# Four graph attention layers on one core: both masks from a transposed adjacency that the host lays beside the first

## What is computed

```python
# layer 0: attention with one head, mask as it is
e = leaky_relu(h @ W.T @ a1 + (h @ W.T @ a2).T); x += elu(softmax(where(adj == 0, -1e9, e)) @ h)
# layer 1: two GAT layers (L1a: 4 heads of 256, elu behind it; L1b: 1 head of 512), softmax over the source
e = leaky_relu(asrc[:, :, None] + adst[:, None, :]); attn = softmax(where(mask, e, -1e9), axis=1)
# layer 2: one head, mask as it is; layer 3: 8 heads of 64 on x @ W_proj, relu behind it
```

## Time and profile before

| | us |
|---|---|
| median of 3 runs (3081.10 to 3087.44) | 3084.61 |
| the profiled execution | 3083.84 |
| its span, first to last instruction | 3082.1 |
| PE busy | 2976.9 (97%) |
| DVE, ACT, POOL busy | 2480.0, 2319.9, 2263.2 |

### The profile page before, as it was taken

One profiled execution on the slowest core, in us unless ns is written; L12 is line 12 of the kernel. 1 busy time (PEld: TensorE's weight loads), 2 busy tenths in 40 slices (PEclk: granted clock), 3 DMA queues, 4 the chain that ended last, 5 costly groups with the idle time before them and its releaser, 6 DMA issues. The chain is left out here.

```text
span 3082.1 us, 79166 instructions
## 1 busy us (share of the span) xinstructions
PE 2976.9 (97%) x21040; PEld 2746.1 (89%) x21040; DVE 2480.0 (80%) x8101; ACT 2319.9 (75%) x6433; POOL 2263.2 (73%) x3214
## 2 busy tenths in 40 slices
PE   7899999999999999999999999999999999999974
PEld 5789999999999999999999999999999999999964
DVE  3578888888888888888888888888888888888852
ACT  2567787778877788777787778877788777787752
POOL 3467777777777777777777777777777777777753
PEclk6999999999999999999999999999999999999985
DMA  5123333333333333333333333333333333333332
GB/s 195 34 69 123 117 119 122 108 124 118 119 123 106 125 117 119 122 109 122 118 119 121 108 122 120 120 118 112 121 120 119 118 110 122 120 120 119 96 107 93
DMA packets 205558, 355.71 MB, mean 115 GB/s; under 512 B 51904, under 2 KB 117568, under 8 KB 188736
## 3 DMA queue, kind: packets, MB, share of 16 engines
q1 hardware_dynamic: 205120, 350.66, 34.8%
HBM read 314.93 MB, written 35.59 MB: 114 GB/s over the span
## 5 line engine op out<-in xcount | busy, mean ns | idle before, releaser
L1454 POOL TENSOR_SCALAR rs<-mv,rs 128x1 f32<-128x1 f32 x512 | 357.6, 698 | 109.2 <-POOL rs L1451 108.8
L997 ACT ACTIVATE eT<-eT,tc 128x128 f32<-128x128 f32 x1024 | 314.1, 389 | 161.3 <-POOL eT L1534 161.3
L432 PE MATMUL bank_b<-w_hi,hT_hi 128*128 128x344 f32 x1536 | 419.8, 328 | 5.6 <-DVE g L1277 3.8
L432 PE MATMUL bank_c<-w_hi,g_hi 128*128 128x258 f32 x2048 | 414.1, 283 | 4.7 <-DVE x L1204 4.7
L432 PE MATMUL bank_c<-w_lo,g_hi 128*128 128x258 f32 x2048 | 414.5, 284 | 0.0
L432 PE MATMUL bank_b<-w_lo,hT_hi 128*128 128x344 f32 x1536 | 408.2, 320 | 0.0
L1329 DVE CUSTOM_DVE_ANT_0 t_all_L<-t_all_L,mask 128x128 f32<-128x128 f32 x1024 | 368.6, 413 | 27.0 <-DMA t_all_L<-t_dram_L 26.5
L432 PE MATMUL bank_b<-w_hi,hT_lo 128*128 128x344 f32 x1536 | 357.0, 327 | 0.0
L432 PE MATMUL bank_c<-w_hi,g_lo 128*128 128x258 f32 x2048 | 351.8, 284 | 0.0
L432 PE MATMUL bank_e<-w_hi,hT_hi 128*128 128x264 f32 x1024 | 341.1, 347 | 5.5 <-DVE out_sb L1372 5.4
L1540 POOL TENSOR_TENSOR eT<-eT,shift_all 128x512 f32<-128x512 f32 x256 | 331.1, 1294 | 4.6 <-ACT eT L997 4.4
(11 more groups left out here) (158 smaller groups left out, 8577.5 us busy)
## 6 DMA issues: line engine op xcount, KB each, us to landing
shift_all<-shift_dram SPq DMA_DIRECT2D x128, 1024.0 KB, 5.3
t_all_L<-t_dram_L SPq DMA_DIRECT2D x128, 512.0 KB, 3.7
x_in<-in_x SPq DMA_DIRECT2D x128, 256.0 KB, 2.6
t_all_L1a<-t_dram_L1a SPq DMA_DIRECT2D x128, 256.0 KB, 3.2
out<-out_sb SPq DMA_DIRECT2D x128, 256.0 KB, 3.1
t_all_L<-t_dram_L SPq DMA_DIRECT2D x256, 64.0 KB, 3.1
adj_in<-in_adj SPq DMA_DIRECT2D x128, 64.0 KB, 3.0
t_dram_L1a<-t_rows_L1a SPq DMA_DIRECT2D x512, 0.5 KB
```

Of the source, the lines that this page charges most:

```text
L432: last = mm(bank[:, 0:width], a[:, c * P:(c + 1) * P], w[:, c, b * width:(b + 1) * width], start=(first and c == chunks[0] and n == 0), st ...
L997: last = activation(eT[:, k, :], eT[:, k, :], ACT.Prelu, bias=tc3[:, k:k + 1], alpha=SLOPE)
L1454: ts(b, mv[layer][:, 0:1], r, -1.0, ALU.mult, ALU.mult).then_inc(sem(f"rs_made{layer}"), 1)
```

## The change

The host stacks the adjacency and its transpose into one array, so that a row of the DMA holds both. `adj_in` and `mask` have two halves, which one `make_mask` fills: half 0 is the mask, half 1 its transpose. A new `turn_mask` on POOL takes the diagonal out of half 1 and writes `mask_turned`; `masked_L3` reads half 1 itself. The two transposes on PE, the two copies on ACT, `identb` and their semaphores are gone. `SKEW` is 11, and the lists of all five engines are put in another order; where a call moves over the end of a step, its graph number changes by one with it (`residual_L0(3)` at the start of a step and `residual_L0(2)` at the end of the one before are the same).

```diff
-SKEW = 12
+SKEW = 11
...
-        identb = sb("identb", [P, P], BF16)
...
-        adj_in = sb("adj_in", [P, XR, P], I32)
-        mask = sb("mask", [P, MR, P], BF16)
+        adj_in = sb("adj_in", [P, XR, 2, P], I32)
+        mask = sb("mask", [P, MR, 2, P], BF16)
         mask_loop = sb("mask_loop", [P, LR, P], BF16)
         mask_turned = sb("mask_turned", [P, TR, P], BF16)
-        mask_flat_turned = sb("mask_flat_turned", [P, PR, P], BF16)
...
                 load(t.graph(0))
-                store(t.graph(12))
                 spread_L2(t.graph(7))
+                send_shift_L3(t.graph(10))
+                send_L1b(t.graph(5))
                 send_L0(t.later_graph(2))
+                spread_shift_L3(t.graph(10))
+                spread_L1b(t.graph(5))
                 spread_L0(t.later_graph(2))
-                send_L1b(t.graph(5))
-                send_shift_L3(t.graph(10))
-                spread_L1b(t.graph(5))
-                spread_shift_L3(t.graph(10))
                 send_L1a(t.graph(3))
+                send_L3(t.graph(9))
                 spread_L1a(t.graph(3))
-                send_L3(t.graph(9))
+                spread_L3(t.graph(9))
+                store(t.graph(11))
                 send_L2(t.graph(6))
-                spread_L3(t.graph(9))
...
-            def turn_mask(t, g):
-                if g.live:
-                    pe.wait_ge(sem("masks_made"), g.made())
-                    if t.full:
-                        pe.wait_ge(sem("x1_made"), g.made())
...
-                    mm(bank_a[:, 0:P], mask_loop[:, g.slot(LR), :], identb[:], start=True, stop=True)\
-                        .then_inc(sem("mask_turned"), 1)
...
-            def turn_mask_L3(t, g):
-                if g.live:
-                    pe.wait_ge(sem("mask_made"), g.made())
-                    if t.full:
-                        pe.wait_ge(sem("mask_copied"), g.made(-7))
...
-                    mm(bank_a[:, 0:P], mask[:, g.slot(MR), :], identb[:], start=True, stop=True)\
-                        .then_inc(sem("flat_turned"), 1)
...
-                project_L1b_first_high(t, t.graph(5))
                 project_L1b_first_low(t, t.graph(5))
+                turn_h3(t, t.graph(9))
                 project_L1b_last(t, t.graph(5))
-                turn_mask(t, t.graph(3))
-                turn_h3(t, t.graph(9))
+                product_L3_last(t, t.graph(11))
                 turn_prob_L1a(t, t.graph(4))
-                product_L3_last(t, t.graph(11))
+                product_L3_first(t, t.graph(11))
                 turn_h1(t, t.graph(3))
-                turn_mask_L3(t, t.graph(10))
                 product_L1a_last(t, t.graph(4))
                 product_L1a_first(t, t.graph(4))
-                product_L3_first(t, t.graph(11))
                 project_L1a_last(t, t.graph(3))
                 turn_exp_L2(t, t.graph(7))
                 project_L3_last_high(t, t.graph(9))
+                project_L3_last_low(t, t.graph(9))
                 product_L2(t, t.graph(7))
-                project_L3_last_low(t, t.graph(9))
                 project_L1a_high(t, t.graph(3))
                 turn_exp_L1b(t, t.graph(5))
+                project_L1a_low(t, t.graph(3))
                 turn_exp_L0(t, t.later_graph(2))
-                project_L1a_low(t, t.graph(3))
                 product_L1b(t, t.graph(5))
+                project_L3_first(t, t.graph(9))
                 product_L0(t, t.later_graph(2))
-                project_L3_first(t, t.graph(9))
+                project_L1b_first_high(t, t.graph(4))
...
-            def copy_mask(g):
-                if g.live:
-                    act.wait_ge(sem("mask_turned"), g.made())
-                    act.wait_ge(sem("L1b_masked"), g.made(TR))
-                    activation(mask_turned[:, g.slot(TR), :], bank_a[:, 0:P], ACT.Copy).then_inc(sem("mask_copied"), 1)
...
-            def copy_mask_L3(g):
-                if g.live:
-                    act.wait_ge(sem("flat_turned"), g.made())
-                    act.wait_ge(sem("L3_masked0"), g.made(PR))
-                    act.wait_ge(sem("L3_masked1"), g.made(PR))
-                    activation(mask_flat_turned[:, g.slot(PR), :], bank_a[:, 0:P], ACT.Copy).then_inc(sem("flat_copied"), 1)
...
-                leaky_L3_first(t.graph(11))
                 leaky_L1a(t.graph(4))
-                norm_0(t.later_graph(2))
-                exp_L1a(t.graph(4))
                 values_L3(t.graph(10))
                 exp_L3_last(t.graph(11))
+                exp_L1a(t.graph(4))
+                hT_hi_L3(t.graph(9))
+                norm_0(t.later_graph(2))
+                exp_L3_first(t.graph(11))
                 norm_1(t.graph(3))
                 pT_L1a(t.graph(4))
-                copy_mask(t.graph(3))
-                hT_hi_L3(t.graph(9))
+                hT_hi_L1a(t.graph(3))
                 leaky_L2(t.graph(7))
-                hT_hi_L1a(t.graph(3))
-                exp_L3_first(t.graph(11))
+                elu_last(t.graph(4))
+                exp_L2(t.graph(7))
                 elu_first(t.graph(4))
-                exp_L2(t.graph(7))
-                copy_mask_L3(t.graph(10))
-                elu_last(t.graph(4))
                 pT_L2(t.graph(7))
-                leaky_L0(t.later_graph(2))
                 g_hi_first(t.graph(4))
-                g_hi_last(t.graph(4))
-                exp_L0(t.later_graph(2))
                 leaky_L1b(t.graph(5))
                 norm_2(t.graph(6))
                 exp_L1b(t.graph(5))
+                g_hi_last(t.graph(4))
+                leaky_L0(t.later_graph(2))
                 pT_L1b(t.graph(5))
+                exp_L0(t.later_graph(2))
                 norm_3(t.graph(8))
                 pT_L0(t.later_graph(2))
                 leaky_L3_last(t.graph(10))
+                leaky_L3_first(t.graph(10))
...
-                residual_L0(t.later_graph(3))
-                stats_1(t.graph(3))
-                moments_3(t.graph(8))
                 moments_1(t.graph(3))
-                stats_2(t.graph(6))
+                targets_L3(t.graph(10))
                 most_L1a(t.graph(4))
-                columns_L0(t.later_graph(2))
-                rows_L0(t.later_graph(2))
-                sources_L3(t.graph(10))
+                most_L3_last(t.graph(10))
                 most_L3_first(t.graph(10))
-                targets_L3(t.graph(10))
                 recip_L1a(t.graph(4))
-                most_L3_last(t.graph(10))
-                rows_L1b(t.graph(5))
-                stats_0(t.later_graph(1))
                 most_leaky_L3(t.graph(10))
                 rows_shift_L3(t.graph(10))
+                hT_lo_L3(t.graph(9))
+                rows_L1b(t.graph(5))
+                columns_L0(t.later_graph(2))
+                moments_3(t.graph(8))
+                values_L1b(t.graph(5))
+                rows_L0(t.later_graph(2))
+                recip_L3(t.graph(11))
+                hT_lo_L1a(t.graph(3))
                 moments_2(t.graph(6))
-                values_L1b(t.graph(5))
-                hT_lo_L3(t.graph(9))
-                hT_lo_L1a(t.graph(3))
                 most_L2(t.graph(7))
-                recip_L3(t.graph(11))
+                stats_0(t.later_graph(0))
                 result_L3(t.graph(11))
+                rows_L1a(t.graph(3))
                 elu_L1a_first(t.graph(4))
-                rows_L1a(t.graph(3))
+                moments_0(t.later_graph(0))
                 elu_L1a_last(t.graph(4))
+                rows_L3(t.graph(9))
+                g_lo_first(t.graph(4))
+                most_L1b(t.graph(5))
+                columns_L2(t.graph(6))
                 most_L0(t.later_graph(2))
+                rows_L2(t.graph(6))
+                recip_L1b(t.graph(5))
                 recip_L2(t.graph(7))
                 residual_L2(t.graph(7))
-                rows_L3(t.graph(9))
-                most_L1b(t.graph(5))
-                moments_0(t.later_graph(1))
                 stats_3(t.graph(7))
-                recip_L0(t.later_graph(2))
-                columns_L2(t.graph(6))
-                g_lo_first(t.graph(4))
-                rows_L2(t.graph(6))
-                recip_L1b(t.graph(5))
                 values_L1a(t.graph(3))
                 residual_L1b(t.graph(5))
+                recip_L0(t.later_graph(2))
+                stats_2(t.graph(5))
+                sources_L3(t.graph(9))
+                residual_L0(t.later_graph(2))
+                stats_1(t.graph(2))
...
-                    pool.wait_ge(sem("flat_turned"), g.made(MR))
-                    ts(mask[:, g.slot(MR), :], adj_in[:, s, :], BIG, -BIG, ALU.mult, ALU.add).then_inc(sem("mask_made"), 1)
+                    ts(mask[:, g.slot(MR), :, :], adj_in[:, s, :, :], BIG, -BIG, ALU.mult, ALU.add).then_inc(sem("mask_made"), 1)
 
             def make_mask_loop(g):
                 if g.live:
                     pool.wait_ge(sem("mask_made"), g.made())
-                    pool.wait_ge(sem("mask_turned"), g.made(LR))
```

(31 more changed lines are left out.)

41 lines of the change are left out of this document (9 added, 32 removed).

## The result

The changed kernel takes **3180.5 us** (median of four, 3177.4 to 3189.7) against 3082.9 of the kernel before beside it: a ratio of 1.032, interval 1.030 to 1.035. It is 98 us slower where the forecast was "no change or a hair slower", and outside the range.

A forecast was written before the change was run, and what follows sets the result against it. PE's own row of work, 22.61 us a step, was taken as the bound: 3083.8 - 30 (transposes and a wait gone) + 38 (new wait at turn_h3) - 3 (overlap) = 3089 us; 80% range 3058 to 3128.

The forecast's parts named there:

- So the two give 0.13 to 0.16 a step: Removing the two mask transposes from PE saves 0.13 to 0.16 us a step; 0.16 was taken.
- Its 0.10 goes too: PE's wait of about 0.10 us a step for exp_L3_first disappears if that operation is now early.
- the gain of 0.26: Transposes and the exp_L3_first wait removed from PE: together 0.26 us a step, 30 us over 115 steps.
- The chain of 4.09 us against 3.76: From product_L0 to turn_h3, releasers take 4.09 us, PE's matmuls 3.76: PE waits 0.33 a step, 38 us.
- The order is the dear part: The new order runs turn_h3 2.9 us of matmuls earlier in PE's row, so it waits: 0.33 us a step.
- wrong altogether: Sign that would refute the forecast: PE waiting at turn_prob_L1a or product_L3, counted as ready 0.5 us early.
- The rival through the queue: L1b's spread, behind the shift's on SP, lands up to 2.2 us later, delaying residual_L0: 0.3 a step, 3124; chance 0.18.
- The rival through the lock: DVE's most_L3 maxima collide with POOL's shift_L3, 0.88 us each: 0.3 a step, 3124, with the queue 3150; chance 0.10.
- Covered, unless its last operations come late: POOL's turn_mask and larger make_mask take 0.4 to 0.7 us of 5.0 free; each 0.1 too late costs 11.
- The load's 64 KB, `SKEW`, ACT's copies: Adjacency load growing from 64 to 128 KB: nothing; SKEW 11: under 1 us; two ACT copies removed: nothing by itself.

The follow-up runs named there:

- e10: e5 with two matmuls of the transposes' size and type put back into PE's row, read by nobody: 3054.7 us, steps of 22.42.
- e2: The changed kernel with recip_L2 and residual_L2 moved earlier on DVE, right behind g_lo_first and ahead of most_L1b: 3089.3 us.
- e1: The changed kernel with L1b's spread issued on SP right behind its send, ahead of the shift's spread: 3162.8 us.
- e14: The changed kernel with only recip_L1a moved later on DVE, behind rows_shift_L3: 3120.8 us.
- e4: The kernel before with only the masks' part of the change, all five lists in the old order, SKEW 12: 3119.3 us.
- e8: e4 with POOL's turn_mask moved from behind make_mask_loop to ahead of masked_L1b: 3093.1 us.
- e15: The changed kernel with four moves: L1b's spread first, residual_L2 early, targets_L3 early, recip_L1a late: 3020.9 us.
- e13: The changed kernel with only targets_L3 moved earlier on DVE, right behind residual_L0: 3094.7 us, steps of 22.93 or 22.38.
- e5: The changed kernel with three moves: L1b's spread first, residual_L2 early, targets_L3 early: 3034.1 us.

## Why the prediction was wrong, point by point

- **"So the two give 0.13 to 0.16 a step"**: nearly right, 0.18 to 0.20 (e10).
- **"Its 0.10 goes too", the gain of 0.26**: too small. With the waits at both turns gone the step is 22.22, 0.39 under before. Reading 22.61 as PE's row of work was the slip: PE counted as busy throughout, and 0.19 of it was waiting. The prediction itself says that each `turn_h3` begins when its chain lets it, and yet takes the step for PE's own row.
- **The chain of 4.09 us against 3.76**: right in each link (4.12, 4.11, and 3.74), and e2, where it is the only wait, gives 3089.3, against 3089 forecast. That the time agrees to the microsecond is partly luck: gain and wait are both larger than forecast (0.39 for 0.26, and 0.40, as 22.62 less 22.22, for 0.33), and the two errors cancel.
- **"The order is the dear part"**: this is the step that failed. It followed one PE instruction, `turn_h3`, to its releasers, and no other. `residual_L2` had moved behind seven calls of DVE's row, and `turn_exp_L0`, which writes the bank that it reads, was never costed: its wait stood in the sum at nothing and is 66.6 us in 120 cases. That place is worth 91 us as the order stands (e2). What I named as "wrong altogether" (waits at `turn_prob_L1a` or `product_L3`) didn't come in this kernel.
- **The rival through the queue**: its path was right up to `columns_L2`, its sign came (ACT's `leaky_L1b` waits for `masked_L1b` for 184.8 us in 123 cases), and it was priced at its far end only, `residual_L0`. A little behind `columns_L2` stands the residual that PE waits for. Its landing came 1.5 us later (4.6 for 3.1), within the 2.2 allowed for. Undoing the queue's part gives 18 us (e1), not 35.
- **The rival through the lock**: the collision came, and in nearly every step (122 of 128; mean 971 ns where 167 is the undisturbed one), but at the operation on `shift_cols` right behind the maxima. The maxima themselves gained: the eight stay at 0.29, where their mean was 413 ns in the kernel before. So the collision moved rather than came new, to a place just ahead of a send. It is 0.80 of the 1.4 us that e14 takes out of DVE's row. Queue and lock were added as separate sizes, 3150; they sit in one ring with `recip_L1a`'s wait, which I hadn't seen.
- **"Covered, unless its last operations come late" (POOL's 0.4 to 0.7 us)**: in the old order not covered: 35 us, 22 to 26 of them the collision at the wrong place (e4, e8). In the new order with all four moves nothing of it shows in the step of 22.22. The rest of the 35 goes with `leaky_L3`, which in e8 begins 0.10 us later in the step than in the kernel before, and was not tested.
- **The load's 64 KB, `SKEW`, ACT's copies**: no wait in any trace points to them; not tested alone.

The transposes are thus worth 20 us on PE, and the order decides whether it shows: e15 differs from the change by four moves.

Open: how e14's 60 us divide between the wait and the collision; and whether the meeting of `masked_L1b` and `g_lo_first` alone makes the two lengths of e13 and e14. It sorts their steps, but the landing that decides it also moves `masked_L1b` itself, and in e1 and e5, where the two hardly meet, the landing was moved as well. That all the waits form one ring is the reading that fits the runs best; no single run shows each link.
